# Giving the last batch's rows a buffer of their own, and splitting expert 0's weights at the end of the batch loop

## The chip, the cores and the metric

The kernel runs on one core of one Trainium2 chip. The metric is device time in microseconds (us) for one execution. Before the change the median of three runs is 1091.33 us (1090.57 to 1091.95).

## The reference, cut to what matters

A decoder layer over 16 batches of 256 tokens, width 256, in three sublayers, each followed by a residual and a layer norm: a small recurrent mixer, a cross attention with 8 heads whose queries come from the tokens, and a mixture of 8 experts with capacity 512. The part around the change is the hand-over from the second layer norm to the experts:

```python
x = _layernorm(x + xattn(ctx_1024, x, ...))            # the normalised rows
weights = _router(x, expert_embeddings)                # top 2 of 8, softmax
cap_ones = where(cumsum(weights > 0, axis=0) <= 512, 1, 0)
vals, idx = top_k((weights * cap_ones).T, 512)         # the rows of each expert
inter = relu(einsum('ech,eih->eci', x_flat[idx], first_linear))
out = einsum('eci,ehi->ech', inter, second_linear) * vals
final = zeros.at[idx].add(out)                         # then residual, layer norm
```

## The kernel before, in words

**Two stages.** Stage one is a loop over the batches, written as `body(b, ...)` for each engine, with eight slots `h` (one for each head) in a body. The bodies overlap: body `b` runs the attention of batch `b` ("att"), the mixer of `b + 1` and `b + 2` ("nxt", "aft"), and the second half of batch `b - 1` ("prv"): residual, second layer norm, router and scatter. Most bodies are in a hardware loop. The last four are written out; the last but one, `body(B - 1, ...)`, has the last batch's attention and the routing of the batch before it, and the last, `body(B, ...)`, has only what is left: the last two heads' weighted sums and the routing of the last batch. Stage two goes over the 8 experts and then does the final layer norm.

**Exact products from pairs.** TensorE multiplies in a reduced float format (`F32R`), so each operand `v` is held as `hi = round(v)` and `lo = v - hi`, and a product is three matmuls (`three`, L558 to L560). ScalarE (ACT) writes `hi`, VectorE (DVE) writes `lo` (`minus`, L1089: the subtraction of one tile from another). For an expert's weights this is `parts(e, u)`: on ACT two copies of 1024 columns, L932 and L936; on DVE two subtractions of 1024 columns, whose two inputs are both tiles in the on-chip memory. Expert 0's weights are loaded into `raw` in `body(0)` and split by `parts(0, 0)` after slot 0 of `body(B - 1)`, on both engines (L1037 on ACT, L1459 on DVE). All later splits are in stage two.

**The second half of a batch.** DVE adds the residual into `xb` (L1242, slot 2), takes the statistics (L1248 to L1253). GpSimd (POOL) raises the variance to the power -0.5 into `c_rs` (L1639, slot 3). The normalised rows go into `xrow`, a tile of two times 260 columns: 256 values, and four more for token number, the two weights and the first expert. For all batches but the last POOL writes them (L1645), for the last DVE does (L1453). TensorE transposes them (`x2T`, L683), ACT copies them out (L907), TensorE multiplies by the router's matrix (`dots`, L690). DVE takes the top 2 (L1127, L1130), the masks, the counts and the positions, and for the last batch also the slot numbers `slot_u` (`last_counts`, `last_places`, `last_slots`; the last write is L1293). POOL adds the four columns and issues `scatter`: four indirect DMAs (L1546), each moving 128 rows of `xrow` to the DRAM tensor `slots` at the places that `slot_u` gives. SyncE (SP) stores the 256 columns of `xrow` to `accd` (L519).

**What a buffer's reuse waits for.** `sc_done` counts the scatters' landings (64 for each batch), `x2_st` the stores' (16 each), `slot_set` the writes of `slot_u`, `crs_set` those of `c_rs`, `x2_set` the writes of the rows. Since there is one `xrow`, DVE waits at L1449 and L1450 for the store and the scatter of the batch before, and at L1451 for `c_rs`, ahead of writing the last batch's rows. `slot_u` is a single tile too; nothing waits for the scatter at its own write, since the rows' write, which comes earlier on the same engine, has waited.

**Between the stages.** In `body(B)`, once the last head is projected, SP loads the weights of experts 1 to 3 (L414, six transfers of 512 KB) and behind them issues the last store (L519). Then it waits for the last store and the last scatter (L527, L528) and loads the rows of expert 0 in two pieces (`xsl`, L531) and of expert 1 (L532). TensorE transposes expert 0's rows (L826), ACT and DVE split them (`xparts`, L1046), and the experts' matmuls begin, which also wait for the split weights (`wl_set`). Each engine executes its own instructions in order; indirect DMAs are issued, and their descriptors written, by POOL.

Of the kernel before, what the change touches and what calls it, by code (L numbers as in the profile page):

```python
# [26 lines left out]
P = 128  # L27
B, S, D = 16, 256, 256
# [9 lines left out]
NT = S // P  # L38
# [6 lines left out]
ROW = D + 4  # L45
# [26 lines left out]
def need(eng, sem, value):  # L72

    if isinstance(value, int) and value <= 0:
        return
    eng.wait_ge(sem, value)


def at(b, value):

    return isinstance(b, int) and b == value


def build(nc, x, xT, ctxt, in_w, xp_w, out_w, vecs, vec16, Wq, Wkv, Wo, bo, emb, W1, W2, out):
# [8 lines left out]
    with top:  # L93
# [9 lines left out]
        ident = sb("ident", [P, P])  # L103
# [24 lines left out]
        def s1(name, shape, dt=F32):  # L128
            return sb(name, shape, dt, one)
# [15 lines left out]
        tokf = s1("tokf", [P, NT])  # L145
# [50 lines left out]
        xb = s1("xb", [P, NT, D])  # L196
        c_st = s1("c_st", [P, NT, 6])
        c_mv = s1("c_mv", [P, NT, 2])
        c_vv = s1("c_vv", [P, NT])
        c_rs = s1("c_rs", [P, NT])  # L200
        xrow = s1("xrow", [P, NT, ROW])
        x2T = s1("x2T", [P, KD, S])
        m8 = s1("m8", [P, NT, 8])
        i8 = s1("i8", [P, NT, 8], U32)
        idxf = s1("idxf", [P, NT, 2])
# [4 lines left out]
        wgt = s1("wgt", [P, NT, 2])  # L210
# [132 lines left out]
        def before(place, b, tile, have, had):  # L343

            mine = FLAT[place][3]
            for n in range(place - 1, -1, -1):
                if FLAT[n][3] == mine and FLAT[n][2] in have:
                    return freed(FLAT[n][0], FLAT[n][1], batch_of(FLAT[n][2], b, tile))
            for n in range(len(FLAT) - 1, -1, -1):
                if FLAT[n][3] == mine and FLAT[n][2] in had:  # L350
                    return freed(FLAT[n][0], FLAT[n][1], batch_of(FLAT[n][2], b - 1, 0))
            return None

        def bank(place):
            return ps[:, G0 + FLAT[place][3], :]
# [46 lines left out]
        def _(sp):  # L402
# [78 lines left out]
            def body(b, par, have, had, tile):  # L481
                a = b + 1
                if "aft" in have:
                    need_apart(sp, in_mm, 2 * (b + 2))
                    sp.dma_start(xts[:], xT_d[bass.ds(b + 2, 1)].rearrange("o p k s -> (o p) k s")).then_inc(xT_ld, 16)
                if "nxt" in have:
                    need_apart(sp, xa_set, a)
                    sp.dma_start(xs[:], x_d[bass.ds(a, 1)].rearrange("o p t d -> (o p) t d")).then_inc(x_ld, 16)
                if at(b, 0):
                    sp.wait_ge(wk_lo_set, 4)  # L490
                    sp.wait_ge(cvec_mm, 1)
                    sp.dma_start(w1r, W1[0]).then_inc(w1r_ld, 16)
                    sp.dma_start(w2r, W2[0]).then_inc(w2r_ld, 16)
                if "att" in have:
                    need_apart(sp, av_mm, 8 * b)
                    values(b, 1)
                if "ctx" in have:
                    next_context(tile + 1)
                    keep_context(tile)
                if "nxt" in have:  # L500
                    need_apart(sp, cx_st, 32 * tile + 32)
                    need_apart(sp, k_mm, 8 * b)
                    for d, part in zip(cx_rows, (kv_hi[1 - par], kv_lo[1 - par])):
                        sp.dma_start(ap(part[:, :, S:KEYS]), d[bass.ds(a, 1)].rearrange("o p k t -> (o p) k t")
                                     ).then_inc(kvc_ld, 16)
                if "ctx" in have:
                    keep_values(tile)
                if "nxt" in have:
                    need_apart(sp, vc_st, 32 * tile + 32)
                    need_apart(sp, av_mm, 8 * b + 4)  # L510
                    values(a, 0)
                if at(b, B):
                    sp.wait_ge(wo_mm, 8 * B)
                    sp.wait_ge(cvec_set, 1)
                    expert_weights(range(1, 4), 0)
                if "prv" in have:
                    c = b - 1
                    need(sp, x2_set, 2 * c + 2)
                    sp.dma_start(acc_rows[bass.ds(c, 1)].rearrange("o p t d -> (o p) t d"),  # L519
                                 xrow[:, :, 0:D]).then_inc(x2_st, 16)  # L520

            bodies(sp, body)


# [30 lines left out]
        def _(pe):  # L555
# [56 lines left out]
            def unit(name, idx, bb, par, g, rows=xts):  # L612
# [66 lines left out]
                if name == "x2T":  # L679
                    need(pe, x2_set, 2 * bb + 2)  # L680
                    for k in range(KD):
                        for t in range(NT):
                            last = pe.transpose(g[:, k * S + t * P:k * S + (t + 1) * P],  # L683
                                                xrow[:, t, k * P:(k + 1) * P], ident[:])
                    last.then_inc(x2T_mm, 1)
                if name == "dots":
                    need(pe, x2T_set, bb + 1)
# [157 lines left out]
        def _(act):  # L845
# [149 lines left out]
            def body(b, par, have, had, tile):  # L995
                for h in range(H):
# [35 lines left out]
                        first_tap(b + 2, h // 2 - 2)  # L1032
                    if h == 5 and "prv" in have:
                        second_weight(b - 1)
                    if at(b, B - 1) and h == 0:
                        act.wait_ge(xp_mm, B)
                        parts(0, 0)  # L1037

# [48 lines left out]
        def _(dve):  # L1087
# [193 lines left out]
            def last_slots(b, par, tile):  # L1281

                if not at(b, B):
                    return
                dve.wait_ge(step_set, 5)
                dve.wait_ge(rank_set, B)
                dve.tensor_tensor(slot_a[:], slot_b[:], rank[:], ALU.add).then_inc(step_set, 1)
                dve.scalar_tensor_tensor(out=keep[:], in0=rank[:], scalar=float(CAP), in1=keep[:], op0=ALU.is_le,
                                         op1=ALU.mult).then_inc(step_set, 1)
                dve.wait_ge(step_set, 7)  # L1290
                dve.tensor_tensor(slot_a[:], slot_a[:], keep[:], ALU.mult).then_inc(step_set, 1)
                dve.wait_ge(step_set, 8)
                dve.tensor_tensor(slot_u[:], slot_a[:].rearrange("p t c -> p (t c)"),  # L1293
                                  trash[:].rearrange("p t c -> p (t c)"), ALU.add).then_inc(slot_set, 1)

# [121 lines left out]
            def body(b, par, have, had, tile):  # L1417
                for h in range(H):
# [27 lines left out]
                    steps(b, par, h, "C", have, tile)  # L1446
                    if at(b, B) and h == 3:

                        dve.wait_ge(x2_st, 16 * (B - 1))  # L1449
                        dve.wait_ge(sc_done, 64 * (B - 1))  # L1450
                        dve.wait_ge(crs_set, B)  # L1451
                        for t in range(NT):
                            dve.tensor_scalar(xrow[:, t, 0:D], xb[:, t, :], c_mv[:, t, 0:1], c_rs[:, t:t + 1],  # L1453
                                              ALU.subtract, ALU.mult).then_inc(x2_set, 1)
                    for name, idx, who, place in todo[lead:]:
                        unit(name, idx, batch_of(who, b, tile), par if who == "att" else 1 - par, bank(place))
                    steps(b, par, h, "D", have, tile)
                    if at(b, B - 1) and h == 0:
                        parts(0, 0)  # L1459

            bodies(dve, body)
# [69 lines left out]
        def _(pool):  # L1531
# [8 lines left out]
            pool.affine_select(out=upper[:], in_=ap(upper[:]), compare_op=ALU.is_ge, fill=0.0, base=0,  # L1540
                               pattern=[[1, P]], channel_multiplier=-1).then_inc(const_set, 1)

            def scatter():
                for t in range(NT):
                    for c in range(2):
                        pool.indirect_dma_start(  # L1546
                            slots, bass.IndirectOffsetOnAxis(slot_u[:, 2 * t + c:2 * t + c + 1], 0),
                            xrow[:, t, :], None).then_inc(sc_done, 16)

            STEPS = 11  # L1550

# [72 lines left out]
            def body(b, par, have, had, tile):  # L1624
                for h in range(H):
# [11 lines left out]
                    if h == 3 and "prv" in have:  # L1637
                        need(pool, cstat_set, 5 * b)
                        pool.tensor_tensor(c_rs[:], c_vv[:], powm[:, 0:NT], ALU.pow).then_inc(crs_set, 1)  # L1639

                        need(pool, x2_st, 16 * (b - 1))
                        need(pool, sc_done, 64 * (b - 1))
                        need_apart(pool, crs_set, b)
                        for t in range(0 if at(b, B) else NT):
                            pool.tensor_scalar(xrow[:, t, 0:D], xb[:, t, :], c_mv[:, t, 0:1], c_rs[:, t:t + 1],  # L1645
                                               ALU.subtract, ALU.mult).then_inc(x2_set, 1)
                    if h == 3 and "ctx" in have:
# [5 lines left out]
                    if h == 6 and "prv" in have:  # L1653
# [1 line left out]
                        need(pool, w1_set, b)  # L1655
                        r = 2 + STEPS * (b - 1)
                        if at(b, B):
                            pool.tensor_copy(xrow[:, :, D], tokf[:])
                            pool.tensor_copy(xrow[:, :, D + 3], idxf[:, :, 0])
                            pool.tensor_tensor(wgt[:, :, 1], w2u[:], wgt[:, :, 0], ALU.mult).then_inc(route_step, 1)  # L1660
                            pool.wait_ge(route_step, r + 1)
                            pool.tensor_copy(xrow[:, :, D + 1:D + 3], wgt[:]).then_inc(route_step, 1)
                            pool.wait_ge(route_step, r + 2)
                            pool.wait_ge(slot_set, B)
                            scatter()
                            continue
                        pool.tensor_tensor(wgt[:, :, 1], w2u[:], wgt[:, :, 0], ALU.mult).then_inc(route_step, 1)
                        need_apart(pool, route_step, r + 1)
# [16 lines left out]
                    if h == 7 and "prv" in have and not at(b, B):  # L1685
# [20 lines left out]
                        pool.tensor_copy(slot_u[:], slot_a[:].rearrange("p t c -> p (t c)")).then_inc(slot_set, 1)  # L1706
                        need_apart(pool, slot_set, b)
                        need(pool, init_st, 16 * (E + 1))
                        scatter()

            bodies(pool, body)

# [70 lines left out]
```

## Time and profile before

| | us |
|---|---|
| median of three runs | 1091.33 |
| the profiled execution's own time | 1091.12 |
| its span (first to last instruction) | 1089.4 |
| PE busy | 1005.7 (92%) |
| DVE busy | 804.1 (74%) |
| ACT busy | 663.5 (61%) |
| POOL busy | 522.2 (48%) |

PE is TensorE's matmuls, and SPq the queue of SyncE, which issues the plain DMAs. A row of the timeline gives the start, the time of the whole group, engine and line, operation, output and inputs with their shapes, and in square brackets how long the engine was idle before it and who ended that. A row of windows gives the busy time of each engine in a stretch, the granted TensorE clock as a share of full speed (PEclk), the mean busy share of the DMA engines and what they moved.

### The profile page before, as it was taken

The page shows a single profiled execution, that of the slowest core. Times are in us where ns is not written, and L with a number is a line of the kernel's source. Part 1 is how long each engine was busy: PE and PEld are TensorE (multiplying, and loading weights), DVE is VectorE, ACT ScalarE, POOL GpSimd, SP SyncE. Part 2 cuts the span into 40 slices and gives each one's busy share as a digit, 9 for nine tenths or more (in the row PEclk, how much of TensorE's full clock was granted, in tenths as well). Part 3 has the DMA queues.
Part 4 walks back from the last instruction along what each step waited for, and adds up shares of the span by engine and source line. Part 5 has one row for each costly group of instructions (what it writes and reads, how often), then busy time and mean ns, then how long its engine had stood idle before and what let it go on. Part 6 is the DMA issues. An engine that isn't in the chain of part 4 may idle for free.

```text
span 1089.4 us, 20865 instructions
## 1 busy us (share of the span) xinstructions
PE 1005.7 (92%) x6878; PEld 940.0 (86%) x6878; DVE 804.1 (74%) x2017; ACT 663.5 (61%) x1714; POOL 522.2 (48%) x830
## 2 busy tenths in 40 slices
PE   6899999999999999999999999999999998299970
PEld 4699999999999999999999999999999888189860
DVE  6877777877787778777887788778878675254526
ACT  5576666666666666666666666666675564055525
POOL 5524363645364535453555455545554534225653
PEclk9899999999999999999999999999999999589995
DMA  7372120112011211121112111221112000575448
GB/s 233 133 237 71 33 99 19 62 33 95 24 56 34 92 31 51 37 86 38 47 36 86 45 41 37 71 63 42 37 56 68 22 32 12 188 228 99 67 49 308
DMA packets 60365, 84.46 MB, mean 78 GB/s; under 512 B 13940, under 2 KB 43688, under 8 KB 60264
## 3 DMA queue, kind: packets, MB, share of 16 engines
q1 hardware_dynamic: 52584, 70.46, 19.4%
q0 software_dynamic: 7680, 12.72, 5.8%
q8 instruction: 55, 0.90, 0.3%
q14 instruction: 46, 0.38, 0.1%
HBM read 44.16 MB, written 38.99 MB: 76 GB/s over the span
## 4 chain that ended last, share of the span: by engine, by line
PE 79%; ACT 8%; DVE 6%; issue 3%; DMA 2%; POOL 1%; ACTq 0%; SPq 0%; DVEq 0%; POOLq 0%
PE ps L558 22%; PE ps L560 21%; PE ps L559 21%; PE ps L585 7%; PE ps L652 3%; PE ps L646 3%; ACT prob L1009 1%; DVE nmx L1425 1%; PE ps L690 1%; ACT fx L1081 1%; DVE cv L1147 1%; ACT k_hi L853 1%; PE ps L676 1%; DMA slots<-xrow,slot_u 1%; ACT x2T L907 1%
## 5 line engine op out<-in xcount | busy, mean ns | idle before, releaser
L1635 POOL TENSOR_SCALAR prob<-prob,rinv 128x333 f32<-128x333 f32 x256 | 140.7, 561 | 349.9 <-DVE rinv L1434 349.3
L1004 ACT ACTIVATE oT_hi<-ps 128x256 fp32r<-128x256 f32 x128 | 49.2, 385 | 197.6 <-PE ps L560 197.6
L558 PE MATMUL ps<-kv_lo,w_hi 128*128 128x256 f32 (+1 forms) x512 | 159.5, 312 | 3.2 <-ACT x2T L907 1.1
L560 PE MATMUL ps<-kv_hi,w_hi 128*128 128x256 f32 (+1 forms) x512 | 153.9, 301 | 0.0
L559 PE MATMUL ps<-kv_hi,w_lo 128*128 128x256 f32 (+1 forms) x512 | 153.6, 300 | 0.0
L1009 ACT ACTIVATE prob<-ps,nmx 128x333 f32<-128x333 f32 x256 | 134.9, 537 | 11.3 <-DVE nmx L1425 9.5
L1089 DVE TENSOR_TENSOR pT_lo<-ps,pT_hi 128x512 fp32r<-128x512 f32 (+1 forms) x256 | 130.2, 550 | 0.6 <-ACT pT_hi L1021 0.6
L1425 DVE TENSOR_REDUCE nmx<-ps 128x2 f32<-128x666 f32 x128 | 108.7, 849 | 22.4 <-PE ps L560 21.4
L585 PE MATMUL ps<-ident,prob 128*128 128x128 f32 (+1 forms) x768 | 108.0, 273 | 2.8 <-DVE oT_lo L1089 2.3
L558 PE MATMUL ps<-pT_lo,v_hi 128*128 128x256 f32 (+1 forms) x384 | 108.4, 282 | 0.9 <-DVE pT_lo L1089 0.9
L560 PE MATMUL ps<-pT_hi,v_hi 128*128 128x256 f32 (+1 forms) x384 | 108.4, 282 | 0.0
L559 PE MATMUL ps<-pT_hi,v_lo 128*128 128x256 f32 (+1 forms) x384 | 107.3, 279 | 0.0
L558 PEld LDWEIGHTS ps<-kv_lo,w_hi 128*128 128x128 f32 x512 | 97.5, 190 | 6.8 <-ACT x2T L907 6.0
L585 PEld LDWEIGHTS ps<-ident,prob 128*128 128x128 f32 (+1 forms) x768 | 92.1, 142 | 8.1 <-issue 6.5
L1095 DVE SCALAR_TENSOR_TENSOR k_lo<-ps,vec,k_hi 128x334 fp32r<-128x334 f32 x128 | 72.3, 565 | 35.6 <-ACT k_hi L853 33.6
L559 PEld LDWEIGHTS ps<-kv_hi,w_lo 128*128 128x128 f32 x512 | 97.8, 191 | 0.0
L560 PEld LDWEIGHTS ps<-kv_hi,w_hi 128*128 128x128 f32 x512 | 97.0, 189 | 0.0
L1147 DVE SCALAR_TENSOR_TENSOR cv<-hp,vec,cv 128x256 f32<-128x256 f32 x192 | 93.2, 499 | 1.3 <-ACT cv L915 1.3
L558 PE MATMUL ps<-k_lo,q_hi 128*128 128x334 f32 x256 | 81.6, 319 | 0.8 <-DVE k_lo L1095 0.8
L1719 POOL DMA_INDIRECT accd<-yo,tku x32 | 54.0, 1687 | 58.4 <-ACT yo L1060 51.4
L560 PE MATMUL ps<-k_hi,q_hi 128*128 128x334 f32 x256 | 80.9, 316 | 0.0
L559 PE MATMUL ps<-k_hi,q_lo 128*128 128x334 f32 x256 | 80.9, 316 | 0.0
(227 smaller groups left out, 3014.4 us busy)
## 6 DMA issues: line engine op xcount, KB each, us to landing
wraw<-in_W SPq DMA_DIRECT2D x14, 512.0 KB, 6.5
vcd_hi<-vst_hi SPq DMA_DIRECT2D x10, 512.0 KB, 2.7
vcd_lo<-vst_lo SPq DMA_DIRECT2D x10, 512.0 KB, 3.6
v_hi<-vcd_hi SPq DMA_DIRECT2D x32, 154.0 KB
v_lo<-vcd_lo SPq DMA_DIRECT2D x32, 154.0 KB
slots<-initr SPq DMA_DIRECT2D x8, 520.0 KB, 6.7
xs<-in_x SPq DMA_DIRECT2D x16, 256.0 KB, 4.1
accd<-xrow SPq DMA_DIRECT2D x16, 256.0 KB, 3.1
```

The lines of the kernel that those rows point to most:

```text
L558: pe.matmul(dst, hi1, lo2, start=first, stop=False, skip_group_check=True)
L559: pe.matmul(dst, lo1, hi2, start=False, stop=False, skip_group_check=True)
L560: return pe.matmul(dst, hi1, hi2, start=False, stop=last, skip_group_check=True)
L585: last = pe.transpose(ps[0:r, T0 + j // 2, (j % 2) * S + t * P:(j % 2) * S + t * P + P], prob[:, ring, t, j * P:j * P + r], ident[:])
L1004: act.activation(oT_hi[:, h % 2, :], ps[:, AVB, 0:S], ACT.Copy).then_inc(oTh_set, 1)
L1009: act.activation(prob[:, h % 2, t, 0:KEYS], ps[:, S0 + t, 0:KEYS], ACT.Exp, bias=nmx[:, h % 2, t:t + 1], accum_out=rsum[:, h % 2, t:t + 1] ...
L1089: return dve.tensor_tensor(dst, src, ap(hi), ALU.subtract)
L1095: dve.scalar_tensor_tensor(out=k_lo[:, idx % 2, :], in0=g[:, 0:KCOL], scalar=vec[:, V_BK + idx:V_BK + idx + 1], in1=ap(k_hi[:, idx % 2, :] ...
L1147: op = dve.scalar_tensor_tensor(out=cv[:, ct, :], in0=hp[:, ct, k:k + S], scalar=w, in1=cv[:, ct, :], op0=ALU.mult, op1=ALU.add)
L1425: dve.tensor_reduce(nmx[:, h % 2, :], ps[:, S0:S0 + NT, 0:KEYS], AX.X, ALU.max, negate=True).then_inc(nmx_set, 1)
L1635: pool.tensor_scalar(prob[:, h % 2, t, 0:KEYS], prob[:, h % 2, t, 0:KEYS], rinv[:, h % 2, t:t + 1], 1.0, ALU.mult, ALU.mult).then_inc(norm ...
L1719: pool.indirect_dma_start(accd, bass.IndirectOffsetOnAxis(tku[u][:, s:s + 1], 0), yo[u][:, s, :], None, compute_op=ALU.add).then_inc(add_d ...
```

## The change

There is a second tile for the rows, `xrow_b`. The last batch (`b == B`) uses it everywhere that the others use `xrow`: DVE's write, the transposes, the four extra columns, the scatter and the store (`rows_out(b)` picks it). DVE's two waits ahead of that write are gone; the one for the earlier scatter now stands ahead of the write of `slot_u`. POOL skips the two same waits for the last batch. `parts(0, 0)` is issued after slot 7 of `body(B)` instead of slot 0 of `body(B - 1)`, on ACT and on DVE; on DVE that is right behind `last_slots`.

```diff
+        xrow_b = s1("xrow_b", [P, NT, ROW])
+        def rows_out(b):
+            return xrow_b if b == B else xrow
 # SP, store to accd
-                                 xrow[:, :, 0:D]).then_inc(x2_st, 16)
+                                 rows_out(b)[:, :, 0:D]).then_inc(x2_st, 16)
 # TensorE, unit x2T
-                                                xrow[:, t, k * P:(k + 1) * P], ident[:])
+                                                rows_out(bb + 1)[:, t, k * P:(k + 1) * P], ident[:])
 # ACT, body
-                    if at(b, B - 1) and h == 0:
+                    if at(b, B) and h == 7:
                         act.wait_ge(xp_mm, B)
                         parts(0, 0)
 # DVE, last_slots
                 dve.wait_ge(step_set, 8)
+                dve.wait_ge(sc_done, 64 * (B - 1))
                 dve.tensor_tensor(slot_u[:], slot_a[:]..., trash[:]..., ALU.add).then_inc(slot_set, 1)
 # DVE, body
                     if at(b, B) and h == 3:
-                        dve.wait_ge(x2_st, 16 * (B - 1))
-                        dve.wait_ge(sc_done, 64 * (B - 1))
                         dve.wait_ge(crs_set, B)
                         for t in range(NT):
-                            dve.tensor_scalar(xrow[:, t, 0:D], xb[:, t, :], ...
+                            dve.tensor_scalar(xrow_b[:, t, 0:D], xb[:, t, :], ...
-                    if at(b, B - 1) and h == 0:
+                    if at(b, B) and h == 7:
                         parts(0, 0)
 # POOL, body
+                        if at(b, B):
+                            continue
                         need(pool, x2_st, 16 * (b - 1))
                         need(pool, sc_done, 64 * (b - 1))
...
-                            scatter()
+                            scatter(xrow_b)
```

## Rows read from the trace of the kernel before

**Rows 1.** The page, chain of waits: its shares by engine.
```profile
PE 79%; ACT 8%; DVE 6%; issue 3%; DMA 2%; POOL 1%; ACTq 0%; SPq 0%; DVEq 0%; POOLq 0%
```
**Rows 2.** Windows of 20 us, one between the stages.
```profile
940.00:960.00 20.00, 6.55 (x20) 5.20 (x20) 6.03 (x21) 3.57 (x5) 4.57 (x8) 0.50 0.50 164
```
**Rows 3.** Timeline of ACT, around the split of expert 0's weights.
```profile
880.53 1.05 ACT L936 ACTIVATE w_hi<-raw 128x1024 fp32r<-128x1024 f32 x1
```
**Rows 4.** Timeline of DVE, the same stretch.
```profile
880.67 2.36 DVE L1089 TENSOR_TENSOR w_lo<-raw,w_hi 128x1024 fp32r<-128x1024 f32 x2 [0.26 <-ACT w_hi L932]
882.95 0.85 DVE L1425 TENSOR_REDUCE nmx<-ps 128x2 f32<-128x666 f32 x1
883.71 0.42 DVE L1089 TENSOR_TENSOR oT_lo<-ps,oT_hi 128x256 fp32r<-128x256 f32 x1
```
**Rows 5.** Timeline of PE, the same stretch.
```profile
884.27 0.41 PE L585 MATMUL ps<-ident,prob 128*77 128x128 f32 x2 [1.16 <-DVE oT_lo L1089]
```
**Rows 6.** The chain of waits in order of time: start, us, what.
```profile
890.50 1.14 ACT prob L1009 x4
...
928.19 5.19 DMA slots<-xrow,slot_u
...
946.45 2.86 DMA slots<-xrow,slot_u
949.40 2.78 DMA xsl<-slots
```
**Rows 7.** Timeline of DVE, the last batch's routing.
```profile
930.12 0.17 DVE L1253 TENSOR_SCALAR c_vv<-c_mv 128x2 f32<-128x2 f32 x1
933.47 0.73 DVE L1453 TENSOR_SCALAR xrow<-xb,c_mv,c_rs 128x256 f32<-128x256 f32 x2 [3.18 <-DMA slots<-xrow,slot_u]
941.63 0.16 DVE L1293 TENSOR_TENSOR slot_u<-slot_a,trash 128x4 uint32<-128x4 f32 x1
```
**Rows 8.** Timeline of POOL, the same stretch.
```profile
930.38 0.72 POOL L1639 TENSOR_TENSOR c_rs<-c_vv,powm 128x2 f32<-128x2 f32 x1 [1.23 <-DVE c_vv L1253]
942.56 1.06 POOL L1546 DMA_INDIRECT slots<-xrow,slot_u  x1 [1.53 <-DVE slot_u L1293]
```
**Rows 9.** Timeline of ACT, the same stretch.
```profile
938.86 0.20 ACT L922 ACTIVATE w2u<-dd 128x2 f32<-128x2 f32 x1 [2.79 <-DVE dd L1131]
954.02 1.08 ACT L1046 ACTIVATE xs_hi<-ps 128x512 fp32r<-128x512 f32 x2 [14.96 <-PE ps L826]
```
**Rows 10.** Timeline of SP's queue: when it issued.
```profile
928.39 3.17 SPq L414 DMA_DIRECT2D wraw<-in_W  x6
934.23 0.38 SPq L519 DMA_DIRECT2D accd<-xrow  x1
```
**Rows 11.** Windows of 1 us, the end of the weights' transfers.
```profile
939.00:940.00 1.00, 0.00 (x0) 0.00 (x0) 0.87 (x7) 0.06 (x1) 0.00 (x0) 0.50 0.26 89
```
**Rows 12.** Timeline of POOL, issues elsewhere in the kernel.
```profile
822.67 0.96 POOL L1546 DMA_INDIRECT slots<-xrow,slot_u  x1 [0.30 <-issue]
823.94 1.31 POOL L1546 DMA_INDIRECT slots<-xrow,slot_u  x1 [0.30 <-issue]
...
982.80 1.55 POOL L1719 DMA_INDIRECT accd<-yo,tku  x1 [0.30 <-issue]
984.66 2.27 POOL L1719 DMA_INDIRECT accd<-yo,tku  x1 [0.30 <-issue]
```
**Rows 13.** Timeline of DVE beside the second and the fourth of these.
```profile
823.94 0.47 DVE L1147 SCALAR_TENSOR_TENSOR cv<-hp,vec,cv 128x256 f32<-128x256 f32 x1
...
984.28 2.36 DVE L1089 TENSOR_TENSOR w_lo<-wraw,w_hi 128x1024 fp32r<-128x1024 f32 x2 [4.58 <-ACT w_hi L932]
```
**Rows 14.** Windows of 1 us, where the granted clock (last but two) changed.
```profile
849.00:850.00 1.00, 0.00 (x0) 0.00 (x0) 0.41 (x2) 0.97 (x3) 1.00 (x2) 1.00 0.03 8
...
852.00:853.00 1.00, 1.00 (x7) 1.00 (x7) 0.96 (x6) 0.00 (x0) 0.00 (x0) 0.50 0.00 0
...
960.00:961.00 1.00, 1.00 (x5) 0.83 (x4) 0.28 (x1) 0.00 (x0) 0.00 (x0) 0.82 1.01 414
```

More of the change, by code:

```diff
@@ L1447, in body @@
                     if at(b, B) and h == 3:
-                        dve.wait_ge(x2_st, 16 * (B - 1))
-                        dve.wait_ge(sc_done, 64 * (B - 1))
                         dve.wait_ge(crs_set, B)
                         for t in range(NT):
-                            dve.tensor_scalar(xrow[:, t, 0:D], xb[:, t, :], c_mv[:, t, 0:1], c_rs[:, t:t + 1],
+                            dve.tensor_scalar(xrow_b[:, t, 0:D], xb[:, t, :], c_mv[:, t, 0:1], c_rs[:, t:t + 1],
                                               ALU.subtract, ALU.mult).then_inc(x2_set, 1)
@@ L1541, in _, with scatter @@
                                pattern=[[1, P]], channel_multiplier=-1).then_inc(const_set, 1)
-            def scatter():
+            def scatter(rows):
                 for t in range(NT):
@@ L1547, in scatter @@
                             slots, bass.IndirectOffsetOnAxis(slot_u[:, 2 * t + c:2 * t + c + 1], 0),
-                            xrow[:, t, :], None).then_inc(sc_done, 16)
+                            rows[:, t, :], None).then_inc(sc_done, 16)
             STEPS = 11
@@ L1643, in body @@
                         need_apart(pool, crs_set, b)
-                        for t in range(0 if at(b, B) else NT):
+                        for t in range(NT):
                             pool.tensor_scalar(xrow[:, t, 0:D], xb[:, t, :], c_mv[:, t, 0:1], c_rs[:, t:t + 1],
@@ L1657, in body @@
                         if at(b, B):
-                            pool.tensor_copy(xrow[:, :, D], tokf[:])
-                            pool.tensor_copy(xrow[:, :, D + 3], idxf[:, :, 0])
+                            pool.tensor_copy(xrow_b[:, :, D], tokf[:])
+                            pool.tensor_copy(xrow_b[:, :, D + 3], idxf[:, :, 0])
                             pool.tensor_tensor(wgt[:, :, 1], w2u[:], wgt[:, :, 0], ALU.mult).then_inc(route_step, 1)
                             pool.wait_ge(route_step, r + 1)
-                            pool.tensor_copy(xrow[:, :, D + 1:D + 3], wgt[:]).then_inc(route_step, 1)
+                            pool.tensor_copy(xrow_b[:, :, D + 1:D + 3], wgt[:]).then_inc(route_step, 1)
                             pool.wait_ge(route_step, r + 2)
                             pool.wait_ge(slot_set, B)
-                            scatter()
+                            scatter(xrow_b)
                             continue
@@ L1708, in body @@
                         need(pool, init_st, 16 * (E + 1))
-                        scatter()
+                        scatter(xrow)
             bodies(pool, body)
```

## The prediction

> **What bounds the kernel now.** I read the page's chain of waits first, then the chain in order of time, then each engine's timeline at the places the diff touches. PE holds 79% of the chain [rows 1], so most of the kernel is matmuls, and a saved microsecond elsewhere is worth nothing unless PE was waiting for it. The change touches two places where PE does wait. Between the stages PE is busy 6.55 of 20 us [rows 2]: there the chain is a single file of scatter, rows, router, scatter and load. Inside the heads of the last batch PE hardly pauses, but once it waits 1.16 us for DVE, just behind the split of expert 0's weights [rows 5].
>
> **First part: the weights' split leaves the heads.** In the old place DVE does the two subtractions from 880.67 for 2.36 us. Behind them on DVE stand the row maximum of the next head (882.95) and then `oT_lo` (883.71), in order [rows 4]. PE's last two transposes need `oT_lo` and start at 884.27 after 1.16 us idle [rows 5]. Take the 2.36 us out and the maximum starts about 880.8 (its scores end at 880.7) and `oT_lo` some 2 us earlier, more than PE's pause, so all of the pause goes. The two ACT copies go too (the second is at 880.53 [rows 3]); PE was not waiting for them. Is something else late next? The head's exponentials, its keys' low parts and the next maximum all hang on PE's own stream here, as the chain shows with the exponentials at 890.50 [rows 6] behind PE's weighted sum. They move with PE. I take 1.16 us. The bounds are 0 (the next wait takes its place) and 1.5 us (another small wait shrinks with it).
>
> **Second part: the last rows do not wait for the scatter before.** DVE is idle 3.18 us and starts the rows at 933.47, when the previous scatter lands [rows 7]; that scatter took 5.19 us from its last issue at 928.19 to landing [rows 6]. With `xrow_b` only `c_rs` is left to wait for. POOL writes it from 930.38 for 0.72 us [rows 8], so to 931.10; it could not be earlier, since the variance itself is ready only after 930.12 + 0.17 [rows 7]. With 0.07 us for the hand-over DVE starts at 931.17: 933.47 - 931.17 = 2.30 us. Behind it everything is a chain of dependent short steps up to `slot_u` at 941.63 [rows 7], POOL's first issue at 942.56 [rows 8], the last issue at 946.45 with 2.86 us to landing, and the load of 2.78 us [rows 6]. All of that moves by 2.30. Bounds: 0 if the rows are held by something unseen, 2.4 if the hand-over is free.
>
> **The wait that is added.** DVE now waits for the previous scatter ahead of `slot_u`. That scatter lands at 933.38 (928.19 + 5.19 [rows 6]) and the write comes at 941.63 - 2.30 = 939.33. It has 5.9 us to spare and costs nothing. Queued behind it on DVE are `slot_u`, for which POOL's scatter waits, and the moved split; it costs one for one once the scatter lands after 939.33. The waits that POOL drops for the last batch guarded no work of its own.
>
> **The moved split, on ACT.** The two copies (1.05 us each [rows 3]) now follow `w2u`, which moves to 936.56 and takes 0.20 [rows 9]: about 936.8 to 938.9. ACT's next work, `xs_hi`, comes at 954.02 - 2.3 and it had been idle 14.96 us before it [rows 9]. Free; without this cover it would cost 2.1 us.
>
> **The moved split, on DVE.** It starts right behind `slot_u`, at about 939.45, and ends about 941.8 (2.36 us [rows 4]). DVE has nothing to do before the loaded rows at about 950, so DVE itself loses nothing (2.36 us if that cover were gone). But it now lies beside POOL's scatter, which is on the chain. The trace of before has no such pair in this place, but it has it elsewhere. Adding an expert's result is an indirect DMA issued by POOL in 1.55 us; the one at 984.66 took 2.27 [rows 12], and it started while DVE was in a weights' split that ran from 984.28 [rows 13]. There are six such rows, one per expert that has a split, 2.21 to 2.28 us. The end fits one reading. The first of the two subtractions ends at 984.28 + 1.2 = 985.5, and 985.5 + 1.43 = 986.93, the issue's end. So it stood still from 0.12 us after its start until the first subtraction was over, and the second subtraction did not stop it again. The scatter's own issue shows the same: 0.96 us alone, 1.31 at 823.94 [rows 12], beside a convolution tap of 0.47 us that started with it [rows 13]; 823.94 + 0.47 = 824.41, and 0.84 us later it ends, again 0.12 us of it done before the stop. Twelve batches have such a row.
>
> Now the new place. POOL's first issue starts at 942.56 - 2.30 = 940.26, reaches its point at 940.38, and the first subtraction (939.45 to 940.65) holds it for 0.27 us. The second issue comes 0.30 us after the first has ended (as each does [rows 12]): 940.26 + 1.06 + 0.27 + 0.30 = 941.89, and the second subtraction is over at 941.8. The other two are clear. I take 0.27 us. The bounds are 0 (issue and first subtraction miss each other) and 1.42 (both hold it, 941.8 - 940.38).
>
> The Trainium skill, page "SBUF — State Buffer", section "SBUF: two separate sides", says that DVE and GpSimd have one pair of memory ports in common. A DVE instruction with two inputs in on-chip memory and a GpSimd instruction that reads it exclude each other, and the one that started first keeps the pair for its whole length. That speaks against this change, since the split has two such inputs; the trace agrees with it in kind, by the 2.27 us against 1.55. Read strictly, with the second subtraction taking the pair back at once, it would make the term 1.42 and not 0.27.
>
> **SP's queue.** The weights of experts 1 to 3 are issued at 928.39 for 3.17 us, to 931.56, and the last store follows at 934.23 [rows 10]. It now becomes ready at 931.9 (931.17 + 0.73), so nothing is queued behind anything new. The bulk of these transfers ends by 939.3 [rows 11]. The scatter's first bytes come after the first issue has ended, at 941.6, so its packets still meet an empty queue, with 2 us of margin in place of 4. Were they to meet, the scatter's tail would be 5.19 and not 2.86 [rows 6].
>
> **TensorE's clock.** It is granted at half (1.2 GHz) all through the routing, and rises to full (2.4 GHz) at about 960.4 [rows 14], 4.4 us after the experts' matmuls begin at about 956. The chip decides when; I take the same delay. How large a surprise is: after a pause of PE at 849 to 850 the clock was at half at 852 [rows 14], for about 3.4 us, in which PE did half the work: 1.7 us lost. One such stretch more or less, in the last heads or at the start of the experts, is worth 1.7 us either way.
>
> **The sum.** 1.16 + 2.30 - 0.27 = 3.19 us. The profiled execution took 1091.12 (its span 1089.4 and 1.7 outside), so 1087.93. The median of before lies 0.21 above the profiled one, and I shift by that: 1088.1.
>
> **The rivals.**
>
> *The pause in the heads only moves.* DVE is the second busiest engine and another of its results could be late instead. For: DVE has hardly a gap behind the split [rows 4]. Against: there is just the one pause there, of 1.16 [rows 5]. Gain 2.30 - 0.27 = 2.0: 1089.3.
>
> *The split holds the scatter's issue to its end.* For: the stretched issues [rows 12, 13]. Against: in all six the second subtraction held nothing. Gain 1.16 + 2.30 - 1.42 = 2.0: 1089.3.
>
> *The clock comes out otherwise.* For: its changes hang on pauses, and the change moves pauses [rows 14]. One such stretch more: 3.19 - 1.7 = 1.5: 1089.8. One less: 4.9: 1086.4.
>
> *The earlier scatter runs into the weights: slower than before.* The change moves the scatter 2.3 us towards transfers that do not move. If those still ran when the scatter's packets come, its tail would grow by 5.19 - 2.86 = 2.33, and if they ran until the load of the rows was issued, at about 947, that load would stand behind them too and might double (2.78 more). Then 3.19 - 2.33 - 2.78 = -1.9: 1093.2. It decides against the change only if the transfers end some 7 us later than the 939.3 seen, or the tail and load lose over 3.2 together. Against: the window at 939 to 940 is already down to 89 GB/s [rows 11].
>
> **How the numbers follow.** Forecast 0.65, pause moves 0.10, held to the end 0.08, clock worse 0.08, clock better 0.06, collision 0.03. A measurement of this kernel can tell about 0.2%, 2.2 us, from no change, so the line is at 1089.15. Over it lie the worse clock, about half of the first two rivals, and a small part of the forecast's own spread: faster 0.79, within 0.2% 0.17, slower 0.04. The range takes in the better clock nearly whole, the first two rivals and the worse clock: 1086.6 to 1089.9.
>
> **What would show it.** Right: no PE pause over 0.5 us in the last batch's second head. The rows (`xrow_b`) start 0.1 us after `c_rs`, with DVE idle about 0.9 us before them. `slot_u` does not wait for the scatter. The split lies directly behind `slot_u`, the first issue of the last scatter lasts about 1.3 us and the other three 0.96. The tail of 2.86 and the load of 2.78 are as before. Wrong: a pause on another of DVE's results; issues of 1.3 us or more behind the first; a scatter tail of 4 us or more; half clock inside the last heads.

## The result, and the profile after

Over eight runs of each kernel on one chip the median fell from 1091.80 us (1089.94 to 1092.43) to 1088.14 (1085.10 to 1088.54), a ratio of 0.9962 with a 95% interval of 0.9953 to 0.9971. The medians are 3.7 us apart. The ratio is not their quotient (0.9966) and stands for 4.1 us, with 3.2 to 5.1 inside the interval. The predicted time, 1088.1, was met, but partly by luck: the forecast gain of 3.2 was counted from 1091.33, the median of three runs, and the kernel before had a median of 1091.80 in eight. So the gain itself came out half a microsecond larger than the sum.

The profiled execution of the changed kernel took 1085.10 (span 1082.9), the fastest of the eight. It is 6.0 us under the profiled one of before, and little more than half of that is the change. Where the rest lies is shown below.

**The heads.** The timeline of PE and of DVE (start, length of the group, engine, line, operation), the second head of the last batch:

```profile
880.81 0.82 PE L590 MATMUL ps<-ident,prob 128*128 128x128 f32 x6
```
```profile
879.01 0.85 DVE L1431 TENSOR_REDUCE nmx<-ps 128x2 f32<-128x666 f32 x1 [0.31 <-PE ps L565]
880.49 0.42 DVE L1094 TENSOR_TENSOR oT_lo<-ps,oT_hi 128x256 fp32r<-128x256 f32 x1 [0.63 <-ACT oT_hi L1009]
```

The six transposes now run as one group of 0.82 us. Before, the last two stood alone after 1.16 us of idle PE [rows 5]. DVE is no longer behind: it waits 0.31 us for the scores ahead of the maximum, and 0.63 for ACT ahead of `oT_lo` [rows 4].

**The rows and the scatter.** Timeline of DVE between the stages:

```profile
927.04 0.17 DVE L1258 TENSOR_SCALAR c_vv<-c_mv 128x2 f32<-128x2 f32 x1
928.06 0.73 DVE L1457 TENSOR_SCALAR xrow_b<-xb,c_mv,c_rs 128x256 f32<-128x256 f32 x2 [0.84 <-POOL c_rs L1643]
936.01 0.16 DVE L1296 TENSOR_TENSOR slot_a<-slot_a,keep 128x4 f32<-128x4 f32 x1
936.20 0.16 DVE L1299 TENSOR_TENSOR slot_u<-slot_a,trash 128x4 uint32<-128x4 f32 x1
936.28 2.35 DVE L1094 TENSOR_TENSOR w_lo<-raw,w_hi 128x1024 fp32r<-128x1024 f32 x2
947.70 0.06 DVE L1496 MEMSET ef<- 128x1 f32 x1 [9.06 <-DMA xsl<-slots]
```

The wait ahead of the rows is 0.84 us and ends with `c_rs`; it was 3.18 and ended with the earlier scatter [rows 7]. `slot_u` follows `slot_a` at the usual distance of 0.19 us, so the added wait holds nothing. The split lies where it was expected, and DVE is idle 9.06 us behind it.

POOL and SP in the same stretch:

```profile
927.30 0.72 POOL L1643 TENSOR_TENSOR c_rs<-c_vv,powm 128x2 f32<-128x2 f32 x1 [1.21 <-DVE c_vv L1258]
937.14 1.29 POOL L1550 DMA_INDIRECT slots<-xrow_b,slot_u  x1 [1.60 <-DVE slot_u L1299]
938.74 0.96 POOL L1550 DMA_INDIRECT slots<-xrow_b,slot_u  x1 [0.30 <-issue]
```
```profile
925.31 2.96 SPq L419 DMA_DIRECT2D wraw<-in_W  x6
928.82 0.38 SPq L524 DMA_DIRECT2D accd<-xrow_b  x1
943.98 0.89 SPq L536 DMA_DIRECT2D xsl<-slots  x2
```

The first issue lasts 1.29 us, and was 1.06 [rows 8]: 0.23 us for the neighbour on DVE. Counted from SP's first issue of the weights, which is the end of the heads, the rows start after 2.75 us and started after 5.08 [rows 7, 10]: 2.33 us less.

The chain of waits over the end of the scatter (start, us, what):

```profile
941.27 2.63 DMA slots<-xrow_b,slot_u
...
943.98 2.85 DMA xsl<-slots
```

The tail of the scatter took 2.63 us and the load 2.85; they were 2.86 and 2.78 [rows 6]. So nothing collided. The weights' transfers were down to 25 GB/s in the window of 936 to 937 us, and POOL's first issue ended at 938.43, so about 2 us lay between them. The window of 940 to 960 us has PE busy 11.32 of 20, against 6.55 [rows 2], mostly because the experts' work begins sooner in it:

```profile
940.00:960.00 20.00, 11.32 (x48) 9.33 (x49) 7.21 (x15) 6.35 (x10) 1.92 (x2) 0.63 0.75 269
```

**Where 6.5 us of span come from.** The span can be cut at three events that both timelines have. In us:

| stretch | before | after | less |
|---|---|---|---|
| start to SP's issue of the weights (end of the heads) | 928.39 | 925.31 | 3.08 |
| to the first expert matmul | 27.60 | 25.34 | 2.26 |
| to the last issue of the last expert's results | 102.26 | 101.42 | 0.84 |
| to the end of the span | 31.15 | 30.83 | 0.32 |

The last two, 1.16 us, hold nothing of the change. Nor does most of the first. One window of the changed kernel's batch loop shows it (the granted clock is the last column but two; [rows 14] has the same microsecond of before):

```profile
852.00:853.00 1.00, 1.00 (x11) 1.00 (x10) 0.90 (x6) 0.45 (x2) 0.00 (x0) 1.00 0.00 0
```

TensorE ran this microsecond at full clock (2.4 GHz) and did 11 matmuls in it. In the execution before, after the same pause at 849 to 850, it was at half (1.2 GHz) and did 7. PE's pause there is 1.63 us in both timelines. What remains of the 3.08 without it is read from the heads themselves, below.

### The profile page after: what moved, and what is told of

It is laid out like the page before. It is cut to its first block, busy times and chain, and to the rows that moved or that the text cites. A ratio compares the mean times of both kernels' runs of the same rounds, so it can differ in the third digit from the quotient of the medians.

```text
span 1082.9 us, 20863 instructions
## 1 busy us (share of the span) xinstructions
PE 1000.7 (92%) x6878; PEld 935.4 (86%) x6878; DVE 804.7 (74%) x2017; ACT 662.5 (61%) x1714; POOL 521.6 (48%) x830
## 4 chain that ended last, share of the span: by engine, by line
PE 79%; ACT 8%; DVE 7%; issue 3%; DMA 1%; POOL 1%; ACTq 0%; SPq 0%; DVEq 0%; POOLq 0%
PE ps L563 22%; PE ps L565 21%; PE ps L564 21%; PE ps L590 7%; PE ps L657 3%; PE ps L651 3%; ACT prob L1014 1%; DVE nmx L1431 1%; PE ps L695 1%; ACT fx L1086 1%; DVE cv L1152 1%; ACT k_hi L858 1%; DVE gt L1123 1%; PE ps L681 1%; ACT x2T L912 1%
```

## The experiments

Seven kernels, on two occasions, each with a chip of its own: experiments 1, 2, 3 and 7, then 4, 5 and 6. Within each, the kernels shared the chip and its runs of the kernel before (median 1091.18 of 16, then 1090.90 of 21). "Under before" is the difference of medians. The ratios beside it are not their quotients and stand for 0 to 0.9 us more. What happens at the disputed place is read from a profile; the times decide only what is larger than a few tenths of a microsecond.

**1. The buffer alone.** The changed kernel with both splits back in their old place:

```diff
-                    if at(b, B) and h == 7:
+                    if at(b, B - 1) and h == 0:
```

> The kernel before with the rows' own buffer and the moved scatter wait alone; expert 0's weights are still split in the old place. My theory (two separate gains, one in the heads and one between the stages): the rows start 0.1 us after c_rs, DVE idle about 0.85 us before them, from SP's issue of the weights to that write 2.75 us (5.08 before), first scatter issue 1.06 us and not 1.29, PE's pause of 1.16 us behind the split still there. Time 2.3 us under before. Rival (the gain is one: DVE's queue as a whole runs freer, and the buffer alone gives little): under 1 us. Rival (the buffer gives nearly all of it, the pause in the heads would have been made up later): 3 us or more.

Measured: 1088.92 us, ratio 0.9977 (0.9964 to 0.9990), 2.3 us under before. Timelines of PE, DVE and POOL:

```profile
882.95 0.60 PE L590 MATMUL ps<-ident,prob 128*128 128x128 f32 x4
884.70 0.41 PE L590 MATMUL ps<-ident,prob 128*77 128x128 f32 x2 [1.15 <-DVE oT_lo L1094]
```
```profile
931.51 0.74 DVE L1457 TENSOR_SCALAR xrow_b<-xb,c_mv,c_rs 128x256 f32<-128x256 f32 x2 [0.84 <-POOL c_rs L1643]
```
```profile
940.59 1.06 POOL L1550 DMA_INDIRECT slots<-xrow_b,slot_u  x1 [1.60 <-DVE slot_u L1299]
```

The pause in the heads is there (1.15 us), the rows wait 0.84 us for `c_rs`, and the issue lasts 1.06. This is the second part of the sum, whole and by itself. From SP's issue of the weights at 928.76 to the rows it is 2.75 us, as expected.

**2. The split's move alone.** The kernel before with the condition of `parts(0, 0)` changed to `at(b, B) and h == 7` on both engines.

> The kernel before with the split moved behind slot_u on both engines and nothing else. My theory: no pause of PE behind the old place, 1.2 to 1.4 us gained there; first issue of the last scatter about 1.3 us in place of 1.06, which takes 0.23 back; the rows still wait about 3.2 us for the earlier scatter. Time 1.0 to 1.2 us under before. Rival (the pause only moves): -0.2 to 0.2 us. With rows_only the two should add up to what the whole change gives on this chip, to 0.3 us; if they fall short by more, the parts need each other.

Measured: 1089.87 us, ratio 0.9987 (0.9978 to 0.9996), 1.3 us under before. PE, then DVE and POOL:

```profile
875.27 0.82 PE L585 MATMUL ps<-ident,prob 128*128 128x128 f32 x6
882.41 0.82 PE L585 MATMUL ps<-ident,prob 128*128 128x128 f32 x6
889.49 0.82 PE L585 MATMUL ps<-ident,prob 128*128 128x128 f32 x6
```
```profile
931.95 0.74 DVE L1453 TENSOR_SCALAR xrow<-xb,c_mv,c_rs 128x256 f32<-128x256 f32 x2 [3.14 <-DMA slots<-xrow,slot_u]
```
```profile
941.04 1.29 POOL L1546 DMA_INDIRECT slots<-xrow,slot_u  x1 [1.53 <-DVE slot_u L1293]
```

No pause is left in the heads, and none has appeared elsewhere. The transposes of the first and of the third of these heads are 889.49 - 875.27 = 14.22 us apart; in the kernel of experiment 1, with the split in between, it was 15.54 (875.84 to 891.38):

```profile
875.84 0.82 PE L590 MATMUL ps<-ident,prob 128*128 128x128 f32 x6
...
891.38 0.81 PE L590 MATMUL ps<-ident,prob 128*128 128x128 f32 x6
```

So the pause is worth 1.32 us, not 1.16. (Between the kernel before and the changed one the same two groups give 15.56 - 14.20 = 1.36 us.) Six transposes in one go take 0.82 us; broken in two by a wait they take 0.60 and 0.41, and that 0.19 is counted as busy. The two parts add up: 2.26 + 1.31 = 3.57 us by the medians, against 3.66 for the whole change in the first set of runs and 3.81 in this one (next). So nothing shows that they need each other, though each of these intervals is about 2 us wide.

**3. The changed kernel again**, beside the others.

> The changed kernel itself, beside the others on one chip. Theory of two separate gains: 2.33 between the stages, 1.36 in the heads, less 0.23 at the scatter's issue, 3.4 to 3.5 us under before. Rival (the surplus of the first result over 3.2 came from the clock, which differs from run to run): 3.1 to 3.2 here. The profiled execution was 6.5 us under before; my theory says that 3 us of that are the clock's changes in stretches that the change does not touch, so this profile should differ from that one by its granted clock, in the batch loop above all.

Measured: 1087.37 us, ratio 0.9961 (0.9948 to 0.9975), 3.8 us under before. The expected 3.4 to 3.5 lies in the interval, and so does the rival's 3.1 to 3.2: these runs can't part them by themselves. The rows can: with 1.32 from experiments 1 and 2, 2.33 from the rows' start and 0.23 from the issue it is 3.4. The expectation on this profile failed in one point. I had said it would differ from the first one in the batch loop above all; it did not. SP issues the weights at 925.49, 0.2 us from the 925.31 of the first, and the window at 852 is at full clock in both. The 2.2 us between the two spans (1085.1 and 1082.9) lie behind: 0.96 more from the first expert matmul to the last issue (102.38 against 101.42), and 0.90 more from there to the end (31.73 against 30.83). Of the 0.96 the clock can explain a half: it rose to full 5.13 us after the first expert matmul, and 4.19 us after it in the first profile, and TensorE does half the work in the 0.94 us between. The rest stays open.

Over all nine profiles, of kernels whose code is the same in that part, the window at 852 us was at half clock, or on its way to it, in six (before, the two parts alone, the two below with DVE's half and the early split, and the one with added subtractions) and at full in three. DVE writes `c_vv` once for each batch. Between the 14th and the 15th of these writes lie both the window at 852 and the place of the pause in the heads, so their distance parts the two (starts in us):

| kernel | 14th write | 15th write | apart | clock at 852 | pause in the heads |
|---|---|---|---|---|---|
| before | 839.07 | 894.53 | 55.46 | half | yes |
| buffer alone (1) | 839.53 | 894.96 | 55.43 | half | yes |
| early split (7) | 838.95 | 893.06 | 54.11 | half | no |
| changed | 838.90 | 891.46 | 52.56 | full | no |
| changed again (3) | 839.10 | 891.68 | 52.58 | full | no |
| one input in PSUM (6) | 840.18 | 892.77 | 52.59 | full | no |

The other three kernels, with half clock and no pause, have 54.08 to 54.11. So the pause is worth about 1.35 us here and the stretch at half clock about 1.55, where the prediction had put 1.7. The 3.08 us up to SP's issue of the weights are the pause, those 1.55 of clock, and 0.17 that lie ahead of the 14th write. Neither of the last two is part of the change.

**4. DVE's half of the split alone.** The kernel before; only DVE's `parts(0, 0)` is moved, ACT's two copies stay in the heads.

> The kernel before with DVE's half of the split moved behind slot_u; ACT's two copies stay in the heads (1.05 us each). My theory (PE's pause comes from DVE's 2.36 us ahead of the maximum and oT_lo): the pause of 1.16 us is gone or under 0.3 us, and the gain in the heads is the same 1.2 to 1.4 us as with both halves moved. Rival (ACT's copies delay the attention's ACT work enough to keep a pause): 0.5 us or more of pause left, waiting on an ACT result.

Measured: 1089.61 us, ratio 0.9985 (0.9975 to 0.9994), 1.3 us under before, as with both halves. Timeline of PE:

```profile
882.35 0.82 PE L585 MATMUL ps<-ident,prob 128*128 128x128 f32 x6
889.42 0.82 PE L585 MATMUL ps<-ident,prob 128*128 128x128 f32 x6
```

The pause is gone although ACT's copies are still there. It was DVE's 2.36 us alone. In the heads, moving ACT's half as well neither gains nor costs: the first and the third of these groups of transposes are 14.19 us apart here and were 14.22 with both halves moved.

**5. Eight subtractions beside the scatter.** The changed kernel; the two subtractions are issued four times over behind `slot_u`, so that all four issues have such a neighbour. The lines left out below are waits on a new semaphore between the subtractions, and a first one for ACT's copies.

```diff
                     if at(b, B) and h == 7:
...
+                        for i in range(3):
...
+                            dve.tensor_tensor(w1_lo[0][:], w1r, ap(w1_hi[0][:]), ALU.subtract)...
...
+                            dve.tensor_tensor(w2_lo[0][:], w2r, ap(w2_hi[0][:]), ALU.subtract)...
...
                         parts(0, 0)
```

> The changed kernel with the two subtractions of the weights' split issued four times over behind slot_u (the same values written again), eight in a row, some 9.4 us beside all four issues of the last scatter. My reading (the issue stands still from 0.12 us after its start until the one subtraction that is then running ends, and the next does not stop it): first issue 1.29 us, second about 1.85, third about 2.05, fourth about 2.0, the scatter later by 2.5 to 3.0 us and so the kernel. Rival (held to the end of DVE's whole run of such instructions): the first issue lasts 7 to 9 us and the kernel is 8 us slower. Rival (no exclusion, the stretch is a fixed cost): issues 1.29, 0.96, 0.96, 0.96.

Measured: 1089.28 us, ratio 0.9985 (0.9974 to 0.9996). That is 1.6 us under before. The changed kernel was 3.8 us under on the other occasion, and the gap of 2.2 is near what the issues below add up to, 0.90 + 1.01 = 1.9 us. The expected 2.5 to 3.0 was too much, by the fourth issue. Timelines of POOL and of DVE:

```profile
938.90 1.29 POOL L1558 DMA_INDIRECT slots<-xrow_b,slot_u  x1 [1.59 <-DVE slot_u L1300]
940.50 1.86 POOL L1558 DMA_INDIRECT slots<-xrow_b,slot_u  x1 [0.30 <-issue]
942.67 1.97 POOL L1558 DMA_INDIRECT slots<-xrow_b,slot_u  x1 [0.30 <-issue]
944.94 0.96 POOL L1558 DMA_INDIRECT slots<-xrow_b,slot_u  x1 [0.30 <-issue]
```
```profile
940.32 1.22 DVE L1467 TENSOR_TENSOR w_lo<-raw,w_hi 128x1024 fp32r<-128x1024 f32 x1
...
942.59 1.22 DVE L1467 TENSOR_TENSOR w_lo<-raw,w_hi 128x1024 fp32r<-128x1024 f32 x1
...
944.97 2.36 DVE L1095 TENSOR_TENSOR w_lo<-raw,w_hi 128x1024 fp32r<-128x1024 f32 x2
```

Expected were 1.29, 1.85, 2.05 and 2.0; measured 1.29, 1.86, 1.97 and 0.96. The first three follow the reading: the second issue, begun at 940.50, ends 0.82 us after the subtraction that began at 940.32 is over (941.54), and the third 0.83 after the one that ends at 943.81. The fourth was missed. There the subtraction began at 944.97, 0.03 us after the issue, and held nothing, while a tap that began together with its issue (at 823.94 both [rows 12, 13]) did. The starting times do not decide this. The kernel before has, in the same scatter as that tap, another one beside the second issue (timelines of POOL and of DVE):

```profile
821.40 0.97 POOL L1546 DMA_INDIRECT slots<-xrow,slot_u  x1 [0.30 <-issue]
```
```profile
821.38 0.47 DVE L1147 SCALAR_TENSOR_TENSOR cv<-hp,vec,cv 128x256 f32<-128x256 f32 x1
```

It is the same kind of tap, with two inputs in on-chip memory, and it began 0.02 us ahead of the issue, yet the issue kept its length. In this trace twelve such second issues, with the tap from 0.03 us ahead to 0.03 us after the issue's start, all took 0.97 or 0.98 us. The twelve stretched fourth issues, 1.29 to 1.40 us, had theirs from 0.02 us ahead to 0.09 us after. So a stop at a fixed point 0.12 us into the issue fits the stretched issues and fails for thirteen others, and what tells the two kinds apart is not known. Both other rivals for this experiment fall: held to the end of DVE's run the first issue would have lasted 7 us or more, and a fixed cost would have left the others at 0.96.

**6. The same with one input in PSUM.** As 5, but the six added subtractions take `ps[:, 4:6, :]`, in the matmuls' accumulation memory (PSUM), as their first input. Their results are overwritten by the last two, the true ones.

> As more_sbuf, but the six added subtractions read their first input from the matmuls' accumulation memory (PSUM) and not from on-chip tile memory (their results are overwritten by the last two, the true ones). My reading (only an instruction with both inputs in tile memory holds POOL's issue): all four issues at their undisturbed lengths, 1.06 and three times 0.96, since the true pair comes after them; the scatter 0.23 us earlier than in the changed kernel. Rival (any busy DVE holds POOL's issue): the issues as in more_sbuf. The split ends later, at about 945.6 on the changed kernel's clock against the loaded rows at 947.7, and costs nothing.

Measured: 1087.70 us, ratio 0.9963 (0.9948 to 0.9979), 3.2 us under before. POOL, and DVE's first two:

```profile
938.42 1.06 POOL L1558 DMA_INDIRECT slots<-xrow_b,slot_u  x1 [1.60 <-DVE slot_u L1300]
939.78 0.96 POOL L1558 DMA_INDIRECT slots<-xrow_b,slot_u  x1 [0.30 <-issue]
```
```profile
937.57 1.22 DVE L1467 TENSOR_TENSOR w_lo<-ps,w_hi 128x1024 fp32r<-128x1024 f32 x1
938.70 1.21 DVE L1469 TENSOR_TENSOR w_lo<-ps,w_hi 128x1024 fp32r<-128x1024 f32 x1
```

The subtractions are as long (1.22 us) and lie on the same issues, and all four issues have their undisturbed length. So a busy DVE alone does not stretch an issue: beside subtractions of two on-chip tiles three of the four were stretched, beside these none.

**7. The split while DVE waits for the router.** The changed kernel; on ACT `parts(0, 0)` comes after slot 3 of the last body, on DVE right behind the writes of `xrow_b`:

```diff
-                    if at(b, B) and h == 7:      # ACT
+                    if at(b, B) and h == 3:
...
                             dve.tensor_scalar(xrow_b[:, t, 0:D], ...).then_inc(x2_set, 1)
+                        parts(0, 0)
...
-                    if at(b, B) and h == 7:      # DVE
-                        parts(0, 0)
```

> The changed kernel with the split earlier: on ACT after slot 3 of the last body, where ACT was idle 6.27 us, on DVE right behind the writes of xrow_b, where DVE was idle 3.96 us for the router's product. My theory (a subtraction of two tiles in on-chip memory holds POOL's issue until it ends): first issue of the last scatter back to 1.06 us, all four unstretched, MAX8 not delayed, 0.23 us under the changed kernel: too little to be told by the times, to be read from the issue's row. Rival (the 0.23 is the cost of another buffer's scatter, not of DVE's work): first issue still 1.29. Rival (the subtractions hold something else in this place, such as MAX8): DVE's wait for the router's product under 1 us and later rows late by over 0.3 us.

Measured: 1086.79 us, ratio 0.9953 (0.9940 to 0.9967), 4.4 us under before. Timelines of DVE and of POOL:

```profile
930.29 2.35 DVE L1094 TENSOR_TENSOR w_lo<-raw,w_hi 128x1024 fp32r<-128x1024 f32 x2
934.19 0.25 DVE L1132 MAX8 m<-ps 128x8 f32<-128x8 f32 x2 [1.55 <-PE ps L695]
```
```profile
938.58 1.06 POOL L1549 DMA_INDIRECT slots<-xrow_b,slot_u  x1 [1.60 <-DVE slot_u L1299]
```

The issue is back at 1.06 us, and DVE still has 1.55 us to spare ahead of the router's maximum. This has the lowest median of all the kernels. The rows show 0.23 us of it; the rest of the 0.58 us under the changed kernel beside it is inside what the two intervals leave open, so that it beats the changed kernel is shown by the row, not by the times. Another 0.14 us in this profile is not the move's: `slot_u` comes 10.75 us after SP's issue of the weights, against 10.89 in experiment 3. The rows' transposes took 0.94 us in place of 1.08, with the granted clock still at 0.85 in the window of 930 to 931.

## Why the prediction was right, step by step

- **The pause in the heads goes, 1.16 us.** Right in kind: experiments 2 and 4 show it gone, and DVE's subtractions as its only cause. The size was off: 1.32 us, since a wait also breaks PE's stream, which its idle time does not count.
- **The rows do not wait, 2.30 us.** Measured 2.33, and 2.3 by the times of experiment 1.
- **The added wait costs nothing.** `slot_u` follows its predecessor after 0.19 us.
- **The split beside the scatter, 0.27 us.** Measured 0.23 (1.29 us against 1.06) in all four kernels that have subtractions of two tiles in this place. The missing 0.04 is the first subtraction's start: 0.08 us after `slot_u`'s, where 0.12 was taken. No effect, and held to the end (1.42), are out for this place. The number was right, but the reading behind it took in only the stretched issues [rows 12, 13]. It left out twelve issues of the same trace that a like tap did not stretch (experiment 5), and by those the term would have been 0. That the stretch carried over to this place was therefore in part luck: the reading gives the size where an issue is stretched, and not whether it is.
- **ACT's copies and SP's queue are free.** In the heads ACT's part is shown by experiment 4. In the new place ACT still waits 13.14 us for PE ahead of `xs_hi`, so the copies delay nothing. The store is issued at 928.82 with no effect on the tail.
- **The sum.** With the measured terms it is 1.32 + 2.33 - 0.23 = 3.4 us where I had 3.19. The measured ratios allow it, and the half microsecond that the first comparison gave beyond the forecast is about half explained by this; the rest can't be told from the spread of the runs.
- **The clock, up to 1.7 us either way.** No rival came true in the medians, but the profiled execution showed this one: about 1.55 us of its lead, where 1.7 was put on such a stretch. The prediction's last paragraph had asked for no half clock inside the last heads, and there was none. "The same delay" up to the rise at the experts was taken as 4.4 us and held in the first profile, 4.19 against 4.36. Over the nine profiles it ran from 3.01 to 5.13, so the term that was put at nothing is worth up to about half a microsecond either way in a single execution.
- **Pause moves, held to the end, collision:** none occurred. The margin between the weights' transfers and the scatter was about 2 us in the profile, as forecast. What happens without it was not tested.

The rule of the Trainium skill that was weighed (page "SBUF — State Buffer", section "SBUF: two separate sides") names the kind of instruction rightly, as far as experiments 5 and 6 show: two inputs in on-chip memory can stretch the issue, and with one in PSUM none was stretched. Its full exclusion is not what the rows show. DVE's subtractions keep their 1.22 us beside the issues, and a subtraction that follows another without a gap does not take its turn before POOL's. Nor was every issue stretched that such an instruction ran beside: the one at 821.40 was not.

## What to carry to other kernels

Look for pairs in the trace of before that have the same two neighbours as the place a step is moved to, even in another stage: their stretch, laid over the new start times, gave a term that no sum of undisturbed lengths has. Collect the pairs that show no stretch as well, since here they were as many. A wait on a reused buffer that sits in a single-file stretch is worth its idle time less what the next wait keeps (here 3.18 us less 0.84); a pause in a dense stretch of matmuls is worth a little more than its idle time. Where a moved step must fill someone's idle time, choose a gap in which nothing on the path is stretched by it: here the wait for the router, not the scatter.

## What the runs showed of the hardware

- An indirect DMA's issue of 0.96 us became 1.86 and 1.97 beside DVE subtractions of two on-chip tiles, and stayed 0.96 beside equally long ones with an input in PSUM. These two ended 0.82 and 0.83 us after the one subtraction that was running when they began. An issue that has 1.06 us undisturbed, the first after a wait, became 1.29.
- A like instruction beside an issue does not always stretch it. In the trace of before, twelve issues with a tap within 0.03 us of their start took 0.97 or 0.98 us, and twelve with one from 0.02 us ahead to 0.09 us after took 1.29 to 1.40.
- The granted TensorE clock fell to half, or did not, after a PE pause of 1.62 to 1.67 us in executions of the same instructions: it fell in six of nine profiles. It moved the end of the batch loop by about 1.55 us. Two profiles of the same kernel (experiment 3 and the first) differed by a further 1.9 us in the expert and last stages. One profile's total is therefore no measure of a change of this size; its stretches are.
